# An LSTM with a mixture of experts: narrow recurrent products and separate fill products, with a new order on VectorE

## The reference, cut to what matters

```python
def step(carry, xw_t):                 # 1024 times, one after the other
    a = xw_t + prev_h @ Wh             # xw = x @ Wx + b, Wh is 256 x 1024
    i, f, o = sigmoid(a[:, :H]), sigmoid(a[:, H:2*H]), sigmoid(a[:, 2*H:3*H])
    g = tanh(a[:, 3*H:])
    next_c = f * prev_c + i * g
    next_h = o * tanh(next_c)
x = x + hs
x = x + moe(x)   # shared: silu(x@w1)*(x@w3)@w2 / 2; routed: gates * gelu(x@w1)@w2; all / 4
```

## Time and profile before

| what | value |
|---|---|
| median of the runs | 2023.9 us |
| the profiled execution's own time | 2023.38 us |
| its span, first to last instruction | 2021.6 us |
| TensorE matmuls busy | 1655.5 us, 82% |
| TensorE weight loads busy | 1456.2 us, 72% |
| VectorE busy | 1619.1 us, 80% |
| ScalarE busy | 806.0 us, 40% |
| GpSimd busy | 135.1 us, 7% |
| mean granted clock of TensorE | 0.997 |

### The profile page before, as it was taken

One profiled execution on the slowest core, in us unless ns is written; L12 is line 12 of the kernel. 1 busy time (PEld: TensorE's weight loads), 2 busy tenths in 40 slices (PEclk: granted clock), 3 DMA queues, 4 the chain that ended last, 5 costly groups with the idle time before them and its releaser, 6 DMA issues. The chain is left out here.

```text
span 2021.6 us, 95636 instructions
## 1 busy us (share of the span) xinstructions
PE 1655.5 (82%) x37356; PEld 1456.2 (72%) x37356; DVE 1619.1 (80%) x14263; ACT 806.0 (40%) x5529; POOL 135.1 (7%) x457
## 2 busy tenths in 40 slices
PE   7888888788888888888888887888888888888888
PEld 6777777777777777777777776777777777777777
DVE  6888788787878878788787877878788787887874
ACT  3554343343433434343343433434334343433432
POOL 0000000000000000000000000000000000000000
PEclk9999999999999999999999999999999999999999
DMA  5000000000000000000000000000000000000000
GB/s 232 3 3 3 3 6 3 6 3 3 6 3 6 3 3 6 3 6 3 6 3 3 6 3 6 3 3 6 3 5 3 4 4 3 6 3 6 3 3 7
DMA packets 7223, 19.85 MB, mean 10 GB/s; under 512 B 1136, under 2 KB 5616, under 8 KB 5872
## 3 DMA queue, kind: packets, MB, share of 16 engines
q1 hardware_dynamic: 6768, 13.73, 1.8%
HBM read 11.63 MB, written 2.10 MB: 7 GB/s over the span
## 5 line engine op out<-in xcount | busy, mean ns | idle before, releaser
L687 PE MATMUL gates<-hh,wh_lo 128*128 128x32 f16 x16384 | 820.7, 194 | 349.1 <-DVE hh L608 346.1
L687 PEld LDWEIGHTS gates<-hh,wh_lo 128*128 128x128 f16 x16384 | 597.9, 98 | 544.5 <-DVE hh L608 541.2
L695 PE MATMUL gates<-hh,wh_hi 128*128 128x32 f16 x16384 | 696.7, 183 | 4.2 <-DVE hh L620 4.2
L578 DVE TENSOR_TENSOR_SCAN gates<-part_fac,gates 128x12 f32<-128x12 f32 x3072 | 395.6, 186 | 262.3 <-PE gates L695 238.7
L330 ACT ACTIVATE gates<-gates 128x4 f32<-128x4 f32 x1024 | 161.8, 158 | 1051.5 <-DVE gates L578 1051.5
L695 PEld LDWEIGHTS gates<-hh,wh_hi 128*128 128x128 f16 x16384 | 572.9, 96 | 6.1 <-DVE hh L620 6.1
L340 ACT ACTIVATE to<-o_sum 128x4 f32<-128x4 f32 x1024 | 212.3, 207 | 116.0 <-DVE o_sum L578 0.8
L605 DVE TENSOR_SCALAR to<-to 128x4 f32<-128x4 f32 x1024 | 175.0, 171 | 71.3
L597 DVE TENSOR_TENSOR_SCAN gates<-gates,addend 128x12 f32<-128x12 f32 x1024 | 194.9, 190 | 0.0
L591 DVE SCALAR_TENSOR_TENSOR addend<-gates,c_now 128x4 f32<-128x4 f32 x1024 | 167.7, 164 | 25.1
L333 ACT ACTIVATE addend<-gates 128x8 f32<-128x8 f32 x1024 | 182.2, 178 | 0.0
(11 more groups left out here) (131 smaller groups left out, 1571.3 us busy)
## 6 DMA issues: line engine op xcount, KB each, us to landing
rw_sb<-rw SPq DMA_DIRECT2D x2, 2048.0 KB, 22.2
sw_sb<-sw SPq DMA_DIRECT2D x3, 1024.0 KB, 13.3
outT<-osb SPq DMA_DIRECT2D x16, 128.0 KB, 2.2
x_sb<-xT SPq DMA_DIRECT2D x1, 1920.0 KB, 9.7
wh_sb<-wh SPq DMA_DIRECT2D x1, 1024.0 KB, 4.7
wx_sb<-wx SPq DMA_DIRECT2D x1, 1024.0 KB, 6.5
x_sb<-xT SPq DMA_DIRECT2D x1, 128.0 KB, 4.8
eye_sb<-eye SPq DMA_DIRECT2D x1, 64.0 KB, 6.0
```

The costliest lines, as they stand in the source:

```text
L578: return v.tensor_tensor_scan(dst, part_fac[:].rearrange("p c j -> p (c j)"), parts[q], 0.0, ALU.mult, ALU.add)
L687: mm(copies(q, m, n)[:, :, :, 0:1], wh_lo[:, c, (q * KC + m) * P:(q * KC + m + 1) * P], again(hh[:, c, :, 1:2], n), start=(m == 0 and c == ...
L695: last = mm(copies(q, m, n)[:, :, :, 0:2], wh_hi[:, c, (q * KC + m) * P:(q * KC + m + 1) * P], again(hh[:, c, :, :], n), start=False, stop ...
```

## The change

- TensorE: `copies` and `again` are gone. Low products move 2 columns and high ones 4. A new `fill()` issues six f16 products of 128 columns each, into a part of the bank `acc_lg` that nobody reads, behind the other work of the step; not in the steps 1, 2, 62 and 63 of tiles 1 to 15. The low products are now ordered G, I, F, with a wait for F's seeds ahead of F, and a wait for O's seeds ahead of O.
- `hh` has its parts outside the batch, so that each part's two columns are adjacent.
- VectorE: the seeds are copied as G and I together, then F by itself, then O by itself. The tail of a step is h_hi, h_now, F's seeds, h_lo, halved c, O's seeds. The sum of o is written to PSUM, in F's bank.
- The split of the next x moves from GpSimd to ScalarE (the high part, behind step 60) and VectorE (the low part in two halves, behind steps 61 and 63).
- Places of helpers in PSUM banks move from column 256 to 384.

```diff
-WIDE = 32
-APART = 16
+FILL = 6
+BESIDE = 384
+SPLIT_HI, SPLIT_LO = 60, (61, 63)
...
-        hh = sb("hh", [P, KC, B, 2], F16)
-        h_lo, h_hi = hh[:, :, :, 0], hh[:, :, :, 1]
+        hh = sb("hh", [P, KC, 2, B], F16)
+        h_lo, h_hi = hh[:, :, 0, :], hh[:, :, 1, :]
...
# VectorE, lstm(s)
-                v.tensor_copy(gif_xw, of_gif(seeds[:, piece % 2, at, 0:O * HC]))
+                v.tensor_copy(gi_xw, of_gi(seeds[:, piece % 2, at, 0:F * HC]))
...
                 v.tensor_tensor(h_now, to1[:], tc, ALU.mult).then_inc(s_own, 1)
+                v.tensor_copy(f_xw, seeds[:, piece % 2, at, F * HC:O * HC]).then_inc(s_seeded, 1)
+                dve.wait_ge(s_own, 2 * s + 2)
+                v.scalar_tensor_tensor(h_lo, h_hi, -LO, by_batch(h_now), ALU.mult, ALU.add).then_inc(s_hlo, 1)
                 ins = v.tensor_scalar(c_now[:], cs[:, :, 2], 0.5, None, ALU.mult)
...
-                v.tensor_copy(o_xw, seeds[:, piece % 2, at, O * HC:GATES])
-                dve.wait_ge(s_own, 2 * s + 2)
-                v.scalar_tensor_tensor(h_lo, h_hi, -LO, by_batch(h_now), ALU.mult, ALU.add).then_inc(s_hlo, 1)
+                v.tensor_copy(o_xw, seeds[:, piece % 2, at, O * HC:GATES]).then_inc(s_seeded, 1)
...
# the split of x: ScalarE and VectorE
+                activation(x_part[0][:], x_sb[:, :, (tile + 2) * TT:(tile + 3) * TT], ACT.Identity, scale=s_xin).then_inc(s_parts, 1)
+                dve.wait_ge(s_parts, tile + 1)
+                ins = v.scalar_tensor_tensor(x_part[1][:, k, :], x_sb[:, k, (tile + 2) * TT:(tile + 3) * TT], s_xin,
+                                             x_part[0][:, k, :], ALU.mult, ALU.subtract)
...
# TensorE
-                        mm(copies(q, m, n)[:, :, :, 0:1], wh_lo[...], again(hh[:, c, :, 1:2], n), ...)
+                        mm(columns(q, m)[:, :, 0], wh_lo[...], hh[:, c, 1, :], ...)
-                        last = mm(copies(q, m, n)[:, :, :, 0:2], wh_hi[...], again(hh[:, c, :, :], n), ...)
+                        last = mm(columns(q, m)[:, :, 0:2].rearrange("p b j -> p j b"), wh_hi[...], hh[:, c, :, :], ...)
+            def fill():
+                for j in range(FILL):
+                    mm(acc_lg[:, BESIDE:BANK], wh_hi[:, 0, j * P:(j + 1) * P], wh_hi[:, 1, 0:BANK - BESIDE], start=False, stop=True,
+                       skip_group_check=True)
...
-            def lstm(s):
+            def lstm(s, tile):
                 pe.wait_ge(s_hhi, s + 1)
-                low(F)
                 low(G)
                 low(I)
+                if s:
+                    pe.wait_ge(s_seeded, 2 * s - 1)
+                elif tile:
+                    pe.wait_ge(s_seeded, 2 * TS - 1)
+                low(F)
                 pe.wait_ge(s_hlo, s + 1)
...
+                if s:
+                    pe.wait_ge(s_seeded, 2 * s)
+                elif tile:
+                    take_back(pe, s_seeded, 2 * TS)
                 low(O)
...
                     mixture(s, True)
+                    if s not in (LOGITS, LOGITS + 1, LAST, LAST + 1):
+                        fill()
```

More of the change, by code:

```diff
@@ L77 @@
 LO_OF = {SCALES + 3 + i: i for i in range(2 * NW)}
-SPLIT_AT = 5
+SPLIT_HI, SPLIT_LO = 60, (61, 63)
 STAGE_AT = 6
@@ L96, in cond_resid_kernel, with beside @@
         parts = [gates[:, q * BANK:q * BANK + HC * PARTS] for q in range(4)]
-        gif_xw = gates.rearrange("p (q n) -> p q n", n=BANK)[:, G:O, 0:HC * PARTS].rearrange(
+        gi_xw = gates.rearrange("p (q n) -> p q n", n=BANK)[:, G:F, 0:HC * PARTS].rearrange(
             "p q (c j) -> p q c j", j=PARTS)[:, :, :, PARTS - 1]
-        o_xw = parts[O].rearrange("p (c j) -> p c j", j=PARTS)[:, :, PARTS - 1]
-        def beside(q, n, at=256):
+        f_xw, o_xw = (parts[q].rearrange("p (c j) -> p c j", j=PARTS)[:, :, PARTS - 1] for q in (F, O))
+        def beside(q, n, at=BESIDE):
             return gates[:, q * BANK + at:q * BANK + at + n]
         g_sum, i_sum, f_sum = (beside(q, HC * PARTS) for q in (G, I, F))
-        fac = beside(I, HC * 3, 288).rearrange("p (c j) -> p c j", j=3)
-        tf = beside(F, HC, 288)
+        fac = beside(I, HC * 3, BESIDE + 32).rearrange("p (c j) -> p c j", j=3)
+        tf, o_sum = beside(F, HC, BESIDE + 32), beside(F, HC * PARTS, BESIDE + 64)
         cs = beside(O, HC * 3).rearrange("p (c j) -> p c j", j=3)
-        tc = beside(O, HC, 288)
+        tc = beside(O, HC, BESIDE + 32)
         xw_first = [xw_next[:, 0:TT], up_rt[:, 0:TT]]
@@ L260, in _ @@
             stage(0, slice(GATES, (HS + 1) * GATES))
[L262 to L269, removed]
             def piece(q, tile):
@@ L299, in _ @@
                     g.partition_all_reduce(wtop[:, 1:3], wmax[:, 1:3], P, RMAX).then_inc(s_top, 1)
-                if q == SPLIT_AT:
-                    split(slice(2 * TT, 3 * TT))
             finish()
@@ L306, in _ @@
                     piece(q, it)
-                    if q == SPLIT_AT:
-                        split(slice((it + 2) * TT, (it + 3) * TT))
                 finish()
@@ L339, in lstm @@
                 act.wait_ge(s_sum, 5 * s + O_OF)
-                activation(to[:], last_of(o_sum[:]), ACT.Tanh, scale=0.5).then_inc(s_tanh, 1)
+                activation(to[:], last_of(o_sum), ACT.Tanh, scale=0.5).then_inc(s_tanh, 1)
                 act.wait_ge(s_sum, 5 * s + C_OF)
@@ L375, in mixture, with split_hi @@
                     activation(ge[:], up_rt[:, 0:RC * TT].rearrange("p (c t) -> p c t", c=RC), ACT.Gelu).then_inc(s_act, 1)
+            def split_hi(tile):
+                activation(x_part[0][:], x_sb[:, :, (tile + 2) * TT:(tile + 3) * TT], ACT.Identity, scale=s_xin).then_inc(s_parts, 1)
             for s in range(TS):
@@ L379, in _ @@
                 first_tile(s)
+                if s == SPLIT_HI:
+                    split_hi(0)
             take_back(act, s_sum, 5 * TS)
@@ L386, in _ @@
                     mixture(s, xw_at)
+                    if s == SPLIT_HI and it < NT - 1:
+                        split_hi(it)
                 take_back(act, s_sum, 5 * TS)
@@ L397, in _, with of_gi @@
             done = [0]
-            def of_gif(columns):
+            def of_gi(columns):
                 return columns.rearrange("p (q c) -> p q c", c=HC)
@@ L471, in _ @@
             dve.wait_ge(s_xwc0, MC + 1)
-            v.tensor_copy(gif_xw, of_gif(xw[:, 0:O * HC]))
+            v.tensor_copy(gi_xw, of_gi(xw[:, 0:F * HC]))
+            v.tensor_copy(f_xw, xw[:, F * HC:O * HC])
             v.tensor_copy(o_xw, xw[:, O * HC:GATES]).then_inc(s_hhi, 1)
@@ L592, in lstm @@
                 dve.wait_ge(s_mul, 4 * s + O_OF)
-                summed(o_sum[:], O).then_inc(s_sum, 1)
+                summed(o_sum, O).then_inc(s_sum, 1)
                 dve.wait_ge(s_scan, 3 * s + 3)
@@ L653, in first_tile, with split_lo @@
                                            wx_slice(wx_part[0], i, 2 * NW), ALU.mult, ALU.subtract).then_inc(s_lo, 1)
+            def split_lo(k, tile):
+                dve.wait_ge(s_parts, tile + 1)
+                ins = v.scalar_tensor_tensor(x_part[1][:, k, :], x_sb[:, k, (tile + 2) * TT:(tile + 3) * TT], s_xin,
+                                             x_part[0][:, k, :], ALU.mult, ALU.subtract)
+                if k == KC - 1:
+                    ins.then_inc(s_xpart, 1)
             for s in range(TS):
@@ L657, in _ @@
                 first_tile(s)
+                if s in SPLIT_LO:
+                    split_lo(SPLIT_LO.index(s), 0)
             round_end()
@@ L663, in _ @@
                     mixture(s, ch)
+                    if s in SPLIT_LO and it < NT - 1:
+                        split_lo(SPLIT_LO.index(s), it)
                 round_end()
@@ L671, in _, with columns @@
             mm = nc.tensor.matmul
[L673 to L680, removed]
+            def columns(q, m):
+                return parts[q][:, m * B * PARTS:(m + 1) * B * PARTS].rearrange("p (b j) -> p b j", j=PARTS)
             def low(q):
-                n = WIDE // B
                 for m in range(KC):
                     for c in range(KC):
-                        mm(copies(q, m, n)[:, :, :, 0:1], wh_lo[:, c, (q * KC + m) * P:(q * KC + m + 1) * P],
-                           again(hh[:, c, :, 1:2], n), start=(m == 0 and c == 0), stop=False, skip_group_check=True)
+                        mm(columns(q, m)[:, :, 0], wh_lo[:, c, (q * KC + m) * P:(q * KC + m + 1) * P], hh[:, c, 1, :],
+                           start=(m == 0 and c == 0), stop=False, skip_group_check=True)
             def high(q):
-                n = WIDE // B // 2
                 for m in range(KC):
                     for c in range(KC):
-                        last = mm(copies(q, m, n)[:, :, :, 0:2], wh_hi[:, c, (q * KC + m) * P:(q * KC + m + 1) * P],
-                                  again(hh[:, c, :, :], n), start=False, stop=True, skip_group_check=True)
-                return last
+                        last = mm(columns(q, m)[:, :, 0:2].rearrange("p b j -> p j b"), wh_hi[:, c, (q * KC + m) * P:(q * KC + m + 1) * P],
```

(12 more changed lines are left out.)

6 lines of the change are left out of this document (2 added, 4 removed).

## The result

The changed kernel took 2545.2 us (median of four runs, 2544.6 to 2546.1), the kernel before 2024.4 us in the same runs: ratio 1.257, interval 1.255 to 1.260. The profiled execution has a span of 2542.8 us. The forecast was 1982 us, in a range of 1938 to 2018.

A forecast was written before the change was run, and what follows sets the result against it. Bound: the ring h_hi, PE, scans, tanh, c scan, tanh, h_hi, 1.90 us a turn. Terms: (-0.065 + 0.005) x 1023 = -61.4, +2, +5.3, +12.7, together -41.4 from 2023.4: 1982 us, range 1938 to 2018.

The forecast's parts named there:

- Narrow products: TensorE's recurrent products: low ones save 0.055 us a step, the last high one ends 10.5 ns earlier; together -0.065 us.
- The rival with products under 20 ns: TensorE's product spacing falls with the columns, to 12 to 15 ns; about 1890 to 1900 us, chance 0.10.
- the low products did not keep their 29.6 ns: Rival on TensorE's low products: their spacing stays at 29.6 ns, the step gains 0.005 us; 2038 us, chance 0.08.
- Order, waits, o's sum: DVE's new order and PE's waits for seeds and h_lo: +0.005 us a step (0 to +0.03); o's sum in PSUM helps.
- DVE's tail: End of DVE's step: mixture work starts 0.10 us later, scans 0.13 late in one step a tile; +2 us (0 to +12).
- The tile boundary and the split: Steps at 15 tile boundaries, DVE last there: longer tail and x's split cost 0.35 us each; +5.3 us (0 to 8).
- the work taken from POOL was on nobody's path: 0: Moving x's split off GpSimd (POOL) was claimed to gain nothing: 0 us.
- hardly ever late: Reading of h_lo (L620) on DVE: products with wh_hi wait only 4 us for it in all.
- The fills: Six products of 54 ns, 0.32 us late in PE's step, end before the next h_hi is wanted: 0 us.
- the uncovered case: Fills that do not fit in PE's idle time: at most 0.32 us a step.
- The clock: TensorE's clock falls at nearly every tile boundary, 14 more falls at 0.91 us each: +12.7 us (0 to two or three times this).
- The rival on the slow side: Clock falls inside the tiles, about 0.9 us per low-clock step, deciding from 60 steps; 2104 us with ten a tile, chance 0.10.

The follow-up runs named there:

- the mixed kernel: The changed kernel with the high products back at 32 columns, low ones narrow, six fills kept: 1993.6 us, ratio 0.985 to the kernel before.
- the kernel of 1967 us: Changed kernel with high products at 32 columns, plus fills before the first step, in the first tile's stall and in steps 1, 2, 62, 63: 1967.2 us.
- the second experiment: The changed kernel with all products back at 32 columns and no fills; new order, waits and split of x stay: 2016.7 us, ratio 0.9965.
- the kernels of 2522 and 2545 us: 2522: the changed kernel plus 36 products of 128 columns on TensorE right before the first step, 2521.9 us; 2545: the changed kernel itself, 2545.2 us.

## Why the prediction was wrong

*Narrow products: right.* The step at 1.00 is 1.84 us. Low ones give 0.049 us (1.903 to 1.854, the mixed kernel), high ones 0.017 (1.854 to 1.837); forecast were 0.055 less 0.005 for the waits, and 0.0105. The rival with products under 20 ns is wrong, the low products did not keep their 29.6 ns, and a start every 26 ns with 2 columns ((0.45 - 0.165)/11 in the kernel of 1967 us) agrees with the rule of the Trainium skill (TensorE: Matmul & The Clock Gate, "Wait — 56ns, not 53.3ns?").

*Order, waits, o's sum: right*, by the second experiment.

*DVE's tail: right in kind, and inside its bounds.* In the kernel of 1967 us the step of the earlier trace rows, step 5 of a tile, takes 1.94 for 1.855: 0.09 us, forecast 0.13. The steps 14, 15 and 20 take 1.91, 1.91 and 1.90, 0.15 more, which the centre did not have: 3.6 us in 15 tiles, forecast 2 (0 to 12).

*The tile boundary and the split: wrong.* The +5.3 us took the 2.24 of one boundary for all 15; the others took 1.90, with room on DVE. There x_lo's instruction (0.34 us) fits in: in the run with the split alone it is 0.55 us from h_lo to the scans with it, and it was 0.56 at the ordinary boundary shown above without it, so the term is near 0. And "the work taken from POOL was on nobody's path: 0" was worth -6 to -7 us: it was on the path in step 49 of each tile, and the 4.2 us of waiting for h_lo, read as "hardly ever late", were its trace.

*The fills: right at full clock only.* "No step is over, so 0" used their 54 ns, and so did the uncovered case, at most 0.32 us. At 0.50 it is 0.64, all of it on the path: the clock's term allowed a fill twice its 54 ns, but in a few steps only.

*The clock: the step that failed.* "I forecast the fall at nearly every boundary, 14 more, at the row's price: +12.7 us." The falls came as forecast where the clock was up: at both boundaries that it reached at 1.00. The price was wrong. The row's 0.91 us holds two slow steps and a return, and the return was work of the 32-column products, which this change takes away. The mixed kernels, with 32 columns in half of the products, still had it, with fills and without; with none of them, in the changed kernel, the return came in two tiles of 15. A fall then costs not 0.91 us but the rest of its tile and often the next ones, 42 us for each whole tile (160.2 us, 117.8 at 1.84 a step), 596 us in all where 12.7 were forecast. And the first fall was at no boundary, but in the second step. The trace before had that one, which the prediction did not count: its level was at 0.50 also at 21 to 24 us, in the first steps, and at 93 to 96 us, behind the stall, and back after about 3 us both times. The rule of the Trainium skill that I had weighed (same page, "HAM oscillation — how this bites in real kernels") speaks of gaps between bursts, with a return each time. It did not bear on these boundaries as I had used it: the waits in its example are far longer than TensorE's 0.87 us here, and the 0.50 of this trace lasts over stretches in which TensorE is 99% busy.

The rival on the slow side had the right cause, the narrow products, but had the clock falling inside the tiles again and again. In the traces it never fell in an ordinary step with fills; it fell at the start, in or behind the stall and at boundaries, and mostly stayed: some 900 steps, where the rival decided at 60 and I expected two a tile.

## What to carry to other kernels

Ask of a clock level two things: what holds it and what brings it back. A trace at full clock shows only the first, and the price of a fall read from it contains a return that the old work paid for. Price a change to TensorE's load once at each level, and set the fills against the path at the lower one, where they take double. Compare the version without fills: at half clock it was as fast as the kernel before. And look whether a late step that a row shows is the rule: one boundary in 15 was late, and the step that was late in every tile stood elsewhere.

## What the runs showed of the hardware that was not expected

- The same instructions ran for over 60 us at 1.00 or at 0.50, by what TensorE did just before them (the kernels of 2522 and 2545 us).
- Narrow f16 products lose little at half clock. Twelve low ones took 0.32 us at 1.00 and 0.35 at 0.50, twelve high ones 0.30 and 0.32. With 32 columns they lose much; in the kernel before, in a step at the lower level (low, high, then O's low):

```profile
92.71 0.78 PE L687 MATMUL gates<-hh,wh_lo 128*128 128x32 f16 x12 [2.17 <-DVE hh L608]
93.30 0.67 PE L695 MATMUL gates<-hh,wh_hi 128*128 128x32 f16 x12
93.79 0.39 PE L687 MATMUL gates<-hh,wh_lo 128*128 128x32 f16 x4
```

  that is 0.59 and 0.49 us. This is why the kernel without fills does at half clock what the old one did at full.
- A DVE instruction on 4 columns lasted 0.60 us instead of 0.15 while a GpSimd instruction ran, and ended 0.02 us behind it, 16 times out of 16.
- One program can take times 165 us apart, where a clock level is lost at a boundary in one execution and not in another (2421 to 2586 us, mean clock 0.638 to 0.545).
